# A graph layer's last gathered tile of each batch made on TensorE by one-hot products, in batches 18 to 39

## The reference

```python
h = relu(layernorm(x))                              # (6250, 96)
ea = edge_attr @ W_edge.T + b_edge                  # (106250, 96)
msg = relu(h[src] + ea)
aggr = segment_sum(msg, dst, 6250)
y = (1 + eps) * h + aggr
out = x + relu(y @ W1.T + b1) @ W2.T + b2
```

## Time and profile before

| | |
|---|---|
| runs of the kernel before | 1233.0, 1233.08, 1234.61 us; median 1233.08 |
| the profiled execution's own time | 1224.89 us |
| its span (first to last instruction) | 1223.1 us |
| mean granted TensorE clock | 0.673 of full speed |
| instructions | 7306 |
| DMA | 93.18 MB, mean 76 GB/s |

### The profile page before, as it was taken

The page is one execution under the profiler, slowest core; times in us unless marked ns, Lnnn a source line. Parts: engine busy times, 40 slices in busy tenths (PEclk is TensorE's granted clock), DMA queues, the critical chain, the costliest instruction groups (busy, mean ns, idle before and its releaser), DMA issues.

```text
span 1223.1 us, 7306 instructions
## 1 busy us (share of the span) xinstructions
PE 496.0 (41%) x1592; PEld 249.7 (20%) x1592; DVE 607.6 (50%) x739; ACT 518.7 (42%) x713; POOL 785.8 (64%) x838
## 2 busy tenths in 40 slices
PE   2143344344344334245343253442534334425358
PEld 2011111222121112012111121120211111112146
DVE  6665544555554445364536345352545363543563
ACT  5134444344433335353435333343535343433434
POOL 6766666666666666575757575766757575757530
PEclk9967766767767766566666665666656666666669
DMA  7523333222223223242323332322423232322212
GB/s 217 148 66 71 83 78 68 67 68 68 67 67 68 68 68 98 56 112 71 81 71 80 72 79 64 72 68 61 101 54 82 63 72 64 71 64 67 47 28 79
DMA packets 51178, 93.18 MB, mean 76 GB/s; under 512 B 17722, under 2 KB 20443, under 8 KB 51136
## 3 DMA queue, kind: packets, MB, share of 16 engines
q0 software_dynamic: 26592, 40.85, 16.1%
q1 hardware_dynamic: 24390, 51.63, 15.6%
q10 hardware_dynamic: 154, 0.24, 0.1%
HBM read 87.85 MB, written 4.80 MB: 76 GB/s over the span
## 4 chain that ended last, share of the span: by engine, by line
another core or an unknown queue 32%; ACT 23%; issue 21%; DVE 13%; PE 6%; DVEq 4%; DMA 1%; SPq 0%; ACTq 0%
ACT edge_blocks L451 17%; ACT msg_parts L458 3%; DVE turn_ps L941 3%; DVE turn_ps L920 3%; PE turn_ps L505 2%; DVEq L834 2%; DVE turn_ps L926 2%; ACT msg_parts L463 2%; DVE msg_parts L955 1%; PE agg_ps L604 1%; PE turn_ps L667 1%; DVEq L836 1%; DVE stats L705 1%; DVE acc L825 1%
## 5 line engine op out<-in xcount | busy, mean ns | idle before, releaser
L375 POOL DMA_INDIRECT gathered<-h_table,src_all x810 | 764.4, 944 | 382.0 <-issue 237.7
L451 ACT COPY edge_blocks<-turn_ps 32x640 f32<-32x640 f32 (+1 forms) x480 | 325.9, 679 | 475.9 <-remote 358.8
L505 PE MATMUL turn_ps<-edge_in,w_edge 97*96 97x512 f32 x398 | 268.2, 842 | 324.2 <-issue 258.8
L926 DVE STREAM_TRANSPOSE turn_ps<-edge_blocks 128x960 f32<-128x960 f32 (+1 forms) x81 | 89.7, 1153 | 216.4 <-ACT edge_blocks L451 115.8
L853 DVE TENSOR_REDUCE sums<-agg_ps 128x192 f32<-128x576 f32 x41 | 30.9, 753 | 319.8 <-remote 319.8
L505 PEld LDWEIGHTS turn_ps<-edge_in,w_edge 97*96 97x96 f32 x398 | 88.6, 234 | 482.9 <-issue 482.9
L604 PE MATMUL agg_ps<-msg_parts,select 128*128 128x288 bf16 x816 | 155.6, 367 | 0.0
L458 ACT ACTIVATE msg_parts<-turn_ps 128x960 bf16<-128x960 f32 (+1 forms) x83 | 79.2, 957 | 157.2 <-DVE turn_ps L941 110.3
L771 DVE TENSOR_TENSOR select<-const_ps,dst_rel 128x2560 bf16<-128x2560 f32 (+1 forms) x43 | 120.8, 2812 | 33.2 <-issue 28.5
L604 PEld LDWEIGHTS agg_ps<-msg_parts,select 128*128 128x128 bf16 x816 | 103.4, 127 | 46.1
L941 DVE TENSOR_TENSOR turn_ps<-turn_ps,gathered 128x960 f32<-128x960 f32 (+1 forms) x83 | 91.1, 1144 | 2.1 <-DVE gathered L760 0.5
(11 more groups left out here) (77 smaller groups left out, 187.9 us busy)
## 6 DMA issues: line engine op xcount, KB each, us to landing
edge_in<-edge_t_dram SPq DMA_DIRECT2D x165, 240.0 KB
gathered<-h_table,src_all POOLq DMA_INDIRECT x810
x_all<-x_dram SPq DMA_DIRECT2D x5, 420.0 KB
h_all<-x_dram SPq DMA_DIRECT2D x10, 210.0 KB
out_dram<-h_all SPq DMA_DIRECT2D x10, 210.0 KB
h_table<-h_all SPq DMA_DIRECT2D x3, 420.0 KB
h_table<-h_all SPq DMA_DIRECT2D x1, 630.0 KB
dst_by_row<-dst_rows_dram SPq DMA_DIRECT2D x1, 480.0 KB, 4.1
```

Source lines behind the costliest of these rows:

```text
L375: nc.gpsimd.indirect_dma_start(out=gathered[c % SLOTS][:, at:at + D], out_offset=None, in_=table, in_offset=bass.IndirectOffsetOnAxis(ap=s ...
L451: last = nc.scalar.copy(blocks[e:e + TURN, :, f:f + TURN], edges[f:f + TURN, :, e:e + TURN])
L505: mm = pe.matmul(turn_ps[0:D, q * BANK:q * BANK + (k1 - k0) * EDGE_TILE], w_edge[:], edge_in[c % SLOTS][:, k0 * EDGE_TILE:k1 * EDGE_TILE], ...
L926: last = nc.vector.transpose(in_flat(c, a, b), flat_rows(edge_blocks, a, b))
```

## The change

In batches 18 to 39 (22 batches) POOL gathers 19 tiles instead of 20. The rows of the batch's last tile are made on the chip: the node table is split once into three bf16 parts, `table_parts` (125 partitions x 50 nodes x 3 x 96), in five pieces during batches 3 to 8, by ACT (high and middle) and DVE (rest and low). For each such tile SP broadcasts its 128 source numbers to 125 partitions (`src_wide`, 512 bytes each), DVE compares them with the node numbers, which lie in PSUM, and writes `hot_rows`, 50 matrices of 125x128 in bf16, in the space of `x_all`. PE multiplies each with its 288 columns of the table, 50 matmuls that sum into `prep_ps`. ACT copies the result to `row_parts`, and DVE adds its three parts up into `gathered`. The compare for batch c+2, the sum for c+1 and the matmuls for c+1 stand in iteration c of their engines' loops. The tail moves from batch 18 to 16, and the memset of the hidden layer's row of ones from batch 16 to 40, since `x_all` is in use until then. Semaphores and assertions are left out below.

```diff
@@ -35,8 +35,9 @@
-HIDDEN_ONES_AT = 16
-TAIL_AT = 18
+TAIL_AT = 16
+PIECE_FROM = 3
+PIECE_COLS = 10

@@ -106,6 +106,22 @@
+    def one_hot(c):
+        return TAIL_AT + 2 <= c < END
+    def one_hots_to(c):
+        return sum(one_hot(b) for b in range(c + 1))
+    def gathered_tiles(c, k0, k1):
+        return k1 - k0 - (one_hot(c) and k0 <= tiles_of[c] - 1 < k1)
+    gathers_to = [[sum(gathered_tiles(b, *groups[b][g]) for b in range(c % SLOTS, c + 1, SLOTS) if g < len(groups[b]))
+                   for g in range(len(groups[c]))] for c in range(BATCHES)]
+    PIECES = N // NODE_PARTS // PIECE_COLS

@@ -158,6 +174,10 @@
+        table_parts = sb("table_parts", [NP, COLS, SPLIT, D], BF16)
+        node_ids = sb("node_ids", [NP, COLS])
+        src_wide = [sb(f"src_wide{b}", [NP, EDGE_TILE], I32) for b in range(2)]
+        row_parts = sb("row_parts", [128, SPLIT * D])

...
@@ -239,6 +270,9 @@
+        ids_ps = const_ps[0:NP, WINDOW:WINDOW + COLS]
+        rows_ps = prep_ps[:, 0:SPLIT * D]
+        hot_rows = x_all[:, 0:COLS * EDGE_TILE // 2].bitcast(BF16).rearrange("p (j e) -> p j e", e=EDGE_TILE)

@@ -349,6 +383,11 @@
             for c in range(SLOTS, BATCHES):
                 sp.wait_ge(edge_done, c - SLOTS + 1)
                 load_edges(c)
+                if c + 1 < BATCHES and one_hot(c + 1):
+                    b, tile = (c + 1) % 2, first_tile[c + 1] + tiles_of[c + 1] - 1
+                    if one_hot(c - 1):
+                        sp.wait_ge(hot_made, one_hots_to(c - 1))
+                    sp.dma_start(src_wide[b][:], src_rows[tile:tile + 1, :].broadcast_to((NP, EDGE_TILE))).then_inc(src_wide_in[b], 16)
                 if X_FROM <= c < X_FROM + BLOCKS:

@@ -369,6 +408,8 @@
+            nc.gpsimd.iota(node_ids[:], [[1, COLS]], base=0, channel_multiplier=COLS,
+                           allow_small_or_imprecise_dtypes=True).then_inc(ids_made, 1)

@@ -396,7 +437,7 @@
-                    for k in range(k0, k1):
+                    for k in range(k0, k0 + gathered_tiles(c, k0, k1)):

...
@@ -462,6 +512,19 @@
+                if 0 < c - PIECE_FROM <= PIECES:
+                    act.wait_ge(table_rest, c - PIECE_FROM)
+                    nc.scalar.copy(table_parts[:, piece(c - PIECE_FROM - 1), 1, :],
+                                   by_cols(x_all, c - PIECE_FROM - 1)).then_inc(table_middle, 1)
+                if 0 <= c - PIECE_FROM < PIECES:
+                    act.wait_ge(h_by_dve, DVE_PARTS)
+                    nc.scalar.copy(table_parts[:, piece(c - PIECE_FROM), 0, :],
+                                   by_cols(h_all, c - PIECE_FROM)).then_inc(table_high, 1)
+                if one_hot(c + 1):
+                    act.wait_ge(rows_done, one_hots_to(c + 1))
+                    if one_hot(c):
+                        act.wait_ge(rows_summed, one_hots_to(c))
+                    nc.scalar.copy(row_parts[:], rows_ps).then_inc(rows_moved, 1)
                 if c == TAIL_AT:

@@ -500,6 +563,8 @@
                             pe.wait_ge(tail_added, 1)
+                        if one_hot(c):
+                            pe.wait_ge(rows_moved, one_hots_to(c))
                     elif q % 2 == 0:

@@ -552,6 +617,14 @@
+            def make_rows(c):
+                pe.wait_ge(table_low, PIECES)
+                pe.wait_ge(hot_made, one_hots_to(c))
+                pe.wait_ge(blocks_moved, c - 1)
+                for j in range(COLS):
+                    mm = pe.matmul(rows_ps, hot_rows[:, j, :], table_parts[:, j, :, :], start=(j == 0), stop=(j == COLS - 1))
+                mm.then_inc(rows_done, 1)

@@ -631,6 +704,8 @@
                     sum_windows(c - 1)
+                if one_hot(c + 1):
+                    make_rows(c + 1)
                 if c + 1 < BATCHES:

@@ -919,6 +994,37 @@
+            def piece(k):
+                return slice(k * PIECE_COLS, (k + 1) * PIECE_COLS)
+            def by_cols(rows, k):
+                return rows[:, k * PIECE_COLS * D:(k + 1) * PIECE_COLS * D].rearrange("p (j f) -> p j f", f=D)
+            def take_rest(k):
+                dve.wait_ge(table_high, k + 1)
+                nc.vector.tensor_tensor(by_cols(x_all, k), by_cols(h_all, k), table_parts[:, piece(k), 0, :],
+                                        ALU.subtract).then_inc(table_rest, 1)
+            def take_low(k):
+                dve.wait_ge(table_middle, k + 1)
+                nc.vector.tensor_tensor(table_parts[:, piece(k), 2, :], by_cols(x_all, k), table_parts[:, piece(k), 1, :],
+                                        ALU.subtract).then_inc(table_low, 1)
+            def make_hot(c):
+                if not one_hot(c - 1):
+                    dve.wait_ge(ids_copied, 1)
+                    dve.wait_ge(table_low, PIECES)
+                dve.wait_ge(src_wide_in[c % 2], 16 * sum(one_hot(b) for b in range(c % 2, c + 1, 2)))
+                nc.vector.tensor_tensor(
+                    hot_rows, src_wide[c % 2][:].unsqueeze(1).broadcast_to((NP, COLS, EDGE_TILE)),
+                    ids_ps.unsqueeze(2).broadcast_to((NP, COLS, EDGE_TILE)), ALU.is_equal).then_inc(hot_made, 1)
+            def sum_rows(c):
+                tile = tiles_of[c] - 1
+                dve.wait_ge(rows_moved, one_hots_to(c))
+                nc.vector.tensor_reduce(gathered[c % SLOTS][:, tile * D:(tile + 1) * D],
+                                        row_parts[:].rearrange("p (k f) -> p f k", k=SPLIT), AX.X, ALU.add).then_inc(rows_summed, 1)

@@ -928,6 +1034,8 @@
             def add_rows(c):
+                if one_hot(c):
+                    dve.wait_ge(rows_summed, one_hots_to(c))
                 if by_feature(c):

@@ -975,9 +1083,16 @@
-                if c == HIDDEN_ONES_AT:
-                    dve.wait_ge(h_by_act, ACT_PARTS)
-                    dve.wait_ge(h_by_dve, DVE_PARTS)
+                if 0 < c - PIECE_FROM <= PIECES:
+                    take_low(c - PIECE_FROM - 1)
+                if 0 <= c - PIECE_FROM < PIECES:
+                    take_rest(c - PIECE_FROM)
+                if one_hot(c + 1):
+                    sum_rows(c + 1)
+                if c + 2 < BATCHES and one_hot(c + 2):
+                    make_hot(c + 2)
+                if c == END:
+                    dve.wait_ge(rows_summed, one_hots_to(END))
                     turn_blocks(c + 1)

@@ -1029,6 +1144,7 @@
+        "src_rows": by_tile(src).T,
```

24 lines of the change are left out of this document (20 added, 4 removed).

## The result

The changed kernel takes 1292.39 us (median of 4 runs, 1290.6 to 1299.05) where the kernel before takes 1233.04 us (4 runs, 1232.31 to 1234.61): a ratio of 1.0489, 95% interval 1.0449 to 1.053. The forecast was 1204.5 us with a range of 1198 to 1226. It had the sign wrong and missed by 88 us. The profiled execution of the changed kernel took 1290.6 us, its span is 1288.8 us, against 1224.89 and 1223.1 before.

The account below looks back on a forecast made before the run. No engine was full; POOL's gather bursts and the hold bound the kernel, 1.405 us per gather. Gathers removed -30.9 and memset +2.3 gave -28.6 us, so 1233.08 became 1204.5 us, range 1198 to 1226.

Parts of the forecast that it names:

- PE.: Fifty new matmuls ahead of the edge features take 6.5 to 11.9 us; chain has 3.0 us to spare, likeliest 0.5.
- the hold: PE's signals are seen late during POOL's gather bursts, until 1.405 us per gather plus 0.30 us after the burst's start.
- Gathers removed: Batches 18 to 39 drop one POOL gather each: 22 x 1.405 = 30.9 us saved, floor 27.5.
- DVE: Compare (7.0 us) and sum of three parts (0.5) before the transposes: 7.5 us more, transposes 3.9 us late after the hold.
- ACT's copy: ACT's copy of the 288 finished columns, ahead of its twelve block moves, takes under 0.69 us.
- Table pieces: Splitting the table on DVE and ACT in batches 3 to 8 costs 0 on the path, 11.6 us if uncovered.
- Memset of ones: DVE's 3.70 us memset, moved to batch 40, makes the end 2.3 us later, bounds 0 and 3.7.
- The rival of single bursts: Two-batch bursts fall to one-batch bursts: 1208 us; chance 0.22, shared with the hold being fixed per batch.
- The hold grows with PE's matmuls: Rival: the hold lengthens 0.098 us per PE matmul, +80 us over 22 batches: 1315 us; chance 0.04.
- Edge_done falls into the hold: Rival: a burst's first edge_done signal is held, ACT idles, 14.2 us more per burst: 1391 us; chance 0.07.
- The chain becomes the bound: Rival: DVE-PE-ACT chain 1 us late per burst, 1215.5 us, worst 1258; chance 0.11 shared with blocked POOL, worst 0.02.
- I am wrong if the pause after 38 gathers exceeds 7 us: Sign against the forecast: POOL's pause behind bursts of 38 gathers, expected at 6.6 us, would exceed 7 us.

Follow-up runs that it names:

- run 4: Changed kernel with only 10 gathers per batch in batches 18 to 39, stale rows standing for the other nine: 1083.54 us, one run.
- run 7: Kernel before, all 20 gathers, plus 30 spare matmuls on constant operands per batch ahead of the edge features in batches 18 to 39: 1236.62 us, one run.
- run 1: Kernel before with 19 of 20 gathers in batches 18 to 39, nothing in place of the missing one: 1203.25 us, ratio 0.9743.
- run 3: Changed kernel with 25 of the 50 one-hot matmuls per batch left out, DVE's and ACT's work unchanged: 1218.74 us, ratio 0.9868.
- run 2: Kernel before, all 20 gathers, plus 50 matmuls on constants per batch in batches 18 to 39 and the tail at batch 16: 1314.46 us, one run.
- run 5: Changed kernel with PE's 50 one-hot matmuls moved between the fourth and fifth pair of edge features: 1674.24 us, ratio 1.3629.
- run 6: As run 5, with DVE's memset of ones moved from iteration 40 to 38: 1673.09 us, ratio 1.3617.
- run 8: Kernel before with 19 gathers and 50 spare matmuls on constants per batch in batches 18 to 39: 1279.83 us, one run.
- run 9: Changed kernel with the 50 matmuls split: 30 ahead of the edge features, 20 between their first and second pair: 1257.34 us, one run.
- run 12: Changed kernel with a 128x128 POOL memset after each gather of a full tile: 1257.26 us, one run.
- run 13: Changed kernel with a 128x256 POOL memset behind each gather of batches 16 to 39: 1227.88 us, ratio 0.9985.
- run 10: Kernel before with a 128x128 POOL memset after each gather of a full tile: 1243.93 us, one run.
- run 15: Kernel before with a 128x256 POOL memset behind every gather of a full tile: 1243.61 us, one run.
- run 11: Kernel before with a 128x512 POOL memset after each gather of a full tile: 1413.83 us, one run.
- run 14: As run 13, with DVE's memset of ones in iteration 38 instead of 40: 1229.96 us, ratio 0.9983.

## Why the prediction was wrong

**The step that failed** is "PE.": "fifty take 6.5 to 11.9 us", of which I made a chain "with 3.0 us to spare, likeliest 0.5". The durations were right: 38 of them took 7.04 us, and all 50 took 8.38 us in run 4, inside the range. Wrong was to lay them end to end as if PE ran freely. The prediction had the hold and its length, but as a lateness of signals alone. In the changed kernel PE is also stopped within the fifty, some 12 matmuls and the first pair of edge features come behind the hold, and POOL's permission is behind that pair: 30.71 us a batch instead of 26.85, 22 x 3.86 = 85 us. The forecast named this queue ("PE waits for the hot rows with the edge features, and so POOL's next permission, behind it") and priced it only for DVE's lateness.

The kernel before did not show it: its 30 matmuls or so a batch run without a standstill, as do 30 more in run 7. But the rows had the hint that PE's records and its signals part: the edge features end at 676.89, and ACT, which waits for them, goes on at 687.32. A hold of that size asks what happens to the work queued in it.

**Point by point.**

- *Gathers removed*, 30.9 us: right in size, its reason not shown. Alone they give 32.6 us (run 1), but only 26.8 of that lie in batches 18 to 39 of the traces, 1.22 us a gather and not 1.405. The prediction's ground for per gather against per batch was weak as well: POOL went on at 1177.03, 1.0 us after the one reckoning and 1.1 us before the other, and it was released there by PE's L526, which had waited 12.12 us for DVE.
- *DVE*, +7.5 us: 6.81 + 0.48 = 7.3 us, and harmless (run 3).
- *ACT's copy*, below 0.69 us: 0.40 us.
- *Table pieces*, 0 on the path, by the row beside L794: the price was right in effect, but the row it went by didn't carry over. Six gathers between 155 and 300 us are followed by the next only after 1.78 to 2.17 us instead of 1.25, 3.8 us in all, and each lies beside a subtraction with both operands in SBUF:

```profile
184.26 1.15 DVE L1010 TENSOR_TENSOR table_parts<-x_all,table_parts 125x960 bf16<-125x960 f32 x1
185.33 1.15 DVE L1005 TENSOR_TENSOR x_all<-h_all,table_parts 125x960 f32<-125x960 f32 x1
```

```profile
184.37 1.86 POOL L416 DMA_INDIRECT gathered<-h_table,src_all  x1 [0.30 <-issue]
186.54 0.95 POOL L416 DMA_INDIRECT gathered<-h_table,src_all  x1 [0.30 <-issue]
```

  The gather took 1.86 us instead of 0.95. By the Trainium skill, page "SBUF — State Buffer", section "Who interferes with whom", a VectorE instruction with two SBUF inputs contends with GpSimd reading SBUF; this trace agrees, at 0.5 to 0.9 us a case and not the 1.16 us of the whole subtraction. Little of it reaches the path. On the chip of runs 1 to 4 batch 18 starts at 524.9 and 528.3 us without the pieces and at 527.2 and 525.8 with them; on that of runs 5 to 8 at 520.9 twice without and at 521.1 and 522.4 with. So the pieces cost 1.5 us at most, and the 5.1 us before batch 18 are mostly a matter of the one profiled execution of the kernel before, in which that batch starts earlier (517.9) than in any other trace.
- *Memset of ones*, 2.3 us: more likely its full 3.7, the bound. Behind batch 42's first gather the traces of the changed kernel and of runs 3, 4, 9, 12 and 13, which have it in batch 40, take 47.4 to 47.7 us, those of runs 1, 2, 7, 10 and 15 without it 43.6 to 44.0. Two traces without it don't fit, 46.1 in the kernel before and in run 8 (runs 5, 6, 11 and 14 are left out, with other batch lengths there or the memset moved), and the times settle nothing: moving the memset gave 1.1 us less in one pair of runs and 2.1 us more in the other, both inside their spread.
- *Batches 40 and 41* were taken as unchanged; they cost 4.9 us more, and 3 to 4 in runs 3 and 13 too. It goes with PE's matmuls: fifty spare ones in runs 2 and 8, without the change's other work, cost 4.3 to 4.5 us there, thirty in run 7 0.8.
- *Two-batch bursts*: gone in the changed kernel, in run 3 as well, at 0.33 us a batch there (27.4 against 54.05 / 2). The rival of single bursts was right on that, and small.

**The rivals.** "The hold grows with PE's matmuls", given 0.04 and 1315 us, is the nearest in time of all, 23 us off. It reckoned +3.65 us a batch where +2.46 was measured (30.71 less 28.25), and its law of a fixed price per matmul falls with run 7. "Edge_done falls into the hold" did not happen to the changed kernel, and happened in full in run 5. "The chain becomes the bound" falls with run 4. "I am wrong if the pause after 38 gathers exceeds 7 us" was the right test: it is 7.24 us already after 19.

**Open:** what it is that clears at 1.41 us per gather, since it isn't the gathers' data; whether the hold goes with the gathers or partly with the batches, which bursts of 38 and 40 and run 1 leave open; why it stops PE and not, in these traces, DVE or ACT, whose signals come 0.01 us after their ends; whether the recording of the profile has a part in it, since every run on record has a profile; and which signals get through. In bursts of 38 and 40 an end of edge features 23 to 24 us after the burst's start passed at once, while in bursts of 19 the signals at 9.9 and at 15.5 us waited for the end.

## What to carry to other kernels

When an engine's signals are seen late, ask also whether its own queued work is stopped, and count how much is queued; what fits today may be just below the limit. If the start-to-start time per burst, divided by the number of transfers, stays above the cadence of issue, something clears more slowly than it is issued; check in the DMA packets whether that is the transfers before calling it so. A filler that brings the issue to that slower rate is a cheap experiment that tells such a queue from a dependence, and a signal on the critical path is better placed in a burst's first microseconds: here those given 3 to 4 us in passed at once.

## What the runs showed that I had not expected

- Gathers of 128 rows of 384 bytes are issued every 1.249 us, and their data land some 2.2 us later with no growing delay, yet bursts of 20, 38 and 40 follow each other at 1.41 to 1.42 us a gather.
- In such bursts PE stops in the middle of a series of matmuls that wait for nothing the profile shows, after 34 to 44 of the fifty in the changed kernel, with single ones between gaps of up to 3.0 us; signals of matmuls that ended 9.9 us into a burst of 19 came 17 us later (run 5).
- At a cadence of 1.654 us PE's signals are not late (the fifty matmuls were not tried there); at 1.44 us the standstill is all but gone and PE's signals are still up to 11 us late.
- A gather beside a VectorE subtraction with both operands in SBUF took 1.48 to 1.86 us instead of 0.95; beside the 6.81 us compare, whose one operand is in PSUM, none did.
